# Ten instead of eight feed-forward sums begun in PSUM by VectorE, with new engine orders

## The reference

```
x = x + attn(ln(x))        # q = x Wq'; (q x') x, no softmax
x = x + ffn(ln(x))         # "f1"
x = x + rwkv(ln(x))        # time mix and channel mix
x = x + ffn(ln(x))         # "f2", the same weights as f1

ffn(t):   h = relu(t @ w1[0] + b1[0]);  y = t + h @ w2[0] + b2[0];  return ln(y) * gamma + beta
rwkv(x):  xa = ln(x); k, v, r = mixes of xa with its shift by one token, times Wk, Wv, Wr
          out = sigmoid(r) * wkv(k, v);  u = x + out @ Wo
          xc = ln(u); kk = relu(mix(xc) @ FWk)**2
          return u + sigmoid(mix(xc) @ FWr) * (kk @ FWv)
```

## Time and profile before

| | |
|---|---|
| Time, median of three runs | 259.4 us (259.05 to 259.99) |
| The profiled execution's own time | 259.21 us |
| Its span, first to last instruction | 257.4 us |
| PE busy | 249.5 us, 97% |
| DVE busy | 231.2 us, 90% |
| ACT busy | 231.9 us, 90% |
| POOL busy | 133.2 us, 52% |
| Granted TensorE clock, mean | 0.997 |

### The profile page before, as it was taken

One profiled execution on the slowest core, in us unless ns is written; L12 is line 12 of the kernel. 1 busy time (PEld: TensorE's weight loads), 2 busy tenths in 40 slices (PEclk: granted clock), 3 DMA queues, 4 the chain that ended last, 5 costly groups with the idle time before them and its releaser, 6 DMA issues.

```text
span 257.4 us, 5284 instructions
## 1 busy us (share of the span) xinstructions
PE 249.5 (97%) x1504; PEld 187.8 (73%) x1504; DVE 231.2 (90%) x757; ACT 231.9 (90%) x477; POOL 133.2 (52%) x258
## 2 busy tenths in 40 slices
PE   7899999999999999999999999999999999999991
PEld 7687778768767777668759767757848849778771
DVE  5897999999999999999999999999999995955454
ACT  3789789999999999999999999999999999895741
POOL 1656585944961974044596646636604525340640
PEclk9999999999999999999999999999999999999998
DMA  7932224013022240020763422205204424374297
GB/s 196 308 99 45 42 42 84 0 28 56 3 40 43 41 84 1 0 45 0 134 105 52 74 48 45 42 0 98 67 0 85 81 56 70 55 144 87 45 187 179
DMA packets 17772, 18.10 MB, mean 70 GB/s; under 512 B 1488, under 2 KB 11600, under 8 KB 17744
## 3 DMA queue, kind: packets, MB, share of 16 engines
q0 software_dynamic: 6480, 11.80, 27.0%
q1 hardware_dynamic: 10848, 5.84, 8.1%
q10 hardware_dynamic: 416, 0.14, 0.2%
HBM read 3.87 MB, written 2.10 MB: 23 GB/s over the span
## 4 chain that ended last, share of the span: by engine, by line
PE 94%; DVE 2%; DMA 1%; ACT 1%; POOL 1%; issue 0%; DVEq 0%; POOLq 0%; ACTq 0%
PE bank L1155 21%; PE bank L1164 21%; PE bank L1232 11%; PE bank L1226 11%; PE bank L1114 7%; PE bank L1213 3%; PE bank L1243 3%; PE bank L1197 3%; PE bank L1207 3%; PE bank L1202 3%; PE bank L1142 3%; PE bank L1127 2%; PE bank L1275 1%; DMA R<-in_hidden 1%; PE bank L1175 1%; PE bank L1135 1%
## 5 line engine op out<-in xcount | busy, mean ns | idle before, releaser
L1164 PEld LDWEIGHTS bank<-W,f_h 128*128 128x128 f32 x480 | 58.2, 192 | 8.7 <-issue 8.6
L1155 PE MATMUL bank<-f_yT,W 128*128 128x512 f32 x128 | 61.2, 593 | 0.0
L1164 PE MATMUL bank<-W,f_h 128*128 128x128 f32 x480 | 60.2, 275 | 0.0
L1155 PEld LDWEIGHTS bank<-f_yT,W 128*128 128x128 f32 x128 | 21.9, 190 | 16.3 <-issue 11.3
L1232 PEld LDWEIGHTS bank<-FWv,KK 128*128 128x128 f32 x256 | 30.6, 192 | 3.4 <-issue 2.3
L1226 PE MATMUL bank<-XK,FWk 128*128 128x512 f32 x64 | 32.0, 597 | 0.0
L1232 PE MATMUL bank<-FWv,KK 128*128 128x128 f32 x256 | 31.8, 275 | 0.0
L828 ACT ACTIVATE f_y<-R,f_yn_nb,f_yn_rs 128x128 f32<-128x128 f32 x64 | 26.3, 490 | 0.9 <-POOL f_yn_nb L350 0.9
L895 ACT ACTIVATE f_h<-bank,B 128x512 f32<-128x512 f32 x32 | 21.2, 681 | 5.5 <-PE bank L1155 4.2
L390 POOL DMA_DIRECT2D R<-G x7 | 6.3, 897 | 36.4 <-DVE G L686 36.4
L895 ACT ACTIVATE f_h<-bank,B1C 128x512 f32<-128x512 f32 x32 | 21.4, 682 | 0.1
(11 more groups left out here) (159 smaller groups left out, 620.3 us busy)
## 6 DMA issues: line engine op xcount, KB each, us to landing
R<-BETA POOLq DMA_DIRECT2D x16, 256.0 KB, 3.6
R<-f_zg POOLq DMA_DIRECT2D x14, 256.0 KB, 4.0
R<-N POOLq DMA_DIRECT2D x8, 256.0 KB, 3.4
R<-in_hidden SPq DMA_DIRECT2D x7, 256.0 KB, 5.0
R<-G POOLq DMA_DIRECT2D x7, 256.0 KB, 3.4
out_x<-R SPq DMA_DIRECT2D x7, 256.0 KB, 2.3
W<-in_w SPq DMA_DIRECT2D x2, 256.0 KB, 4.5
BETA<-in_beta SPq DMA_DIRECT2D x1, 256.0 KB, 4.6
```

The costliest lines, as they stand in the source:

```text
L1155: t_.matmul(banks[bank][:], W1[:, n * P:(n + 1) * P], at(f.yT, b)[:], start=True, stop=True).then_inc(f.h_psum[n], 1)
L1164: last = t_.matmul(banks[bank][:, j * C:(j + 1) * C], at(f.h, b)[:, n, j * P:(j + 1) * P], W2[:, n, :], start=False, stop=(n == H - 1), sk ...
```

## The change

`STARTED` gains batch 4 of f1 and batch 3 of f2. So DVE begins ten of the sixteen sums: batches 0 to 4 of f1 and 3 to 7 of f2, the last of them in two halves as before. PE does six `ffn_start` instead of eight. All four written-out lists are new in order, in bank numbers and in the waits for free banks; apart from the two moved `ffn_start` they hold the same calls as before. Two helpers are defined (`norm_bias` on DVE, `norm_log` on ACT) that no list calls. Cut to the lines that the prediction speaks of:

```diff
-STARTED = {"f1": (0, 1, 2, 3), "f2": (4, 5, 6, 7)}
+STARTED = {"f1": (0, 1, 2, 3, 4), "f2": (3, 4, 5, 6, 7)}
...
-            power(1, f1.norm); bias(1, f1.norm); shift(4, na); shift(5, na); power(4, na); ffn_residual(0, f1)
-            bias(4, na); shift(2, f1.norm); power(2, f1.norm); ffn_residual(1, f1); power(5, na); bias(2, f1.norm)
+            power(1, f1.norm); shift(4, na); bias(1, f1.norm); ffn_residual(0, f1); power(4, na); shift(2, f1.norm)
+            ffn_residual(1, f1); power(2, f1.norm); shift(5, na); bias(4, na); bias(2, f1.norm); power(5, na)
...
-            ffn_out(0, f1); tmix_stats(0); mean_var(0, nt); attn_out(3, 2); decay_along_tokens(); ffn_stats(3, f1)
+            mean_var(4, na); bias_rows_centred(); attn_stats(5); attn_out(2, 3); attn_stats(6); decay_along_tokens()
+            ffn_start(0, f1, 1); ffn_stats(2, f1); mean_var(2, f1.norm); ffn_start(1, f1, 0, (f1.h_ready[0], 1))
+            mean_var(5, na); z_stats(0, f1, 1); mean_var(0, f1.znorm); ffn_gain(0, f1, 1); ffn_out(0, f1)
+            tmix_stats(0); mean_var(0, nt); attn_stats(7); attn_out(3, 5); ffn_stats(3, f1); mean_var(6, na)
...
+            ffn_start(4, f1, 2); first_values(1, 4); numerator_sum(1); denominator_sum(1); attn_out(6, 5); weighted(1)
...
+            gate_sum(6); z_stats(1, f2, 5); mix_v(7); gate_log(6, 2); running_max(7, 1); mean_var(1, f2.znorm)
+            cmix_gated(4, 0); gated(6); ffn_start(3, f2, 2, square[2].done(5, "relu")); differences(7, 1)
...
-            attn_transpose(0, 0); attn_gram(0, 1); attn_proj(0, 1); attn_apply(0, 1); attn_transpose(1, 0)
+            attn_gram(0, 0); attn_transpose(0, 1); attn_proj(0, 0); attn_apply(0, 0); attn_transpose(1, 1)
...
+            product_v(6, 6); cmix_down(4, 0, 0); ffn_down(2, f2, 0, 7); product_r(6, 2); ffn_down(2, f2, 1, 7)
+            ffn_down(2, f2, 2, 7); cmix_transpose(5, 4); cmix_down(4, 1, 0); tmix_transpose(7, 6, (m2_ready, 7))
+            cmix_down(4, 2, 0); cmix_down(4, 3, 0); ffn_down(2, f2, 3, 7); cmix_up(5, 1, 6, (xa_ready, 8))
+            cmix_up(5, 3, 3, cgate.done(4, "rl")); cmix_up(5, 0, 4)
+            ffn_transpose(3, f2, 6, square[1].done(5, "relu")); product_k(7, 1); cmix_up(5, 2, 2, gate.done(6, "rl"))
...
+            product_o(7, 4, square[1].done(6, "relu")); gate_product(6, 6, square[3].done(6, "relu"))
+            hidden_up(4, f2, 3, 0, square[2].done(6, "relu")); cmix_down(6, 0, 4, (u1_ready, 8)); cmix_down(6, 1, 4)
+            cmix_down(6, 2, 4); ffn_down(4, f2, 0, 5); cmix_down(6, 3, 4); cmix_transpose(7, 6, cgate.done(6, "rl"))
+            ffn_down(4, f2, 1, 5); ffn_down(4, f2, 2, 5); ffn_down(4, f2, 3, 5); cmix_up(7, 2, 0)
```

More of the change, by code:

```diff
@@ L769, in _ @@
[L769 to L787, removed]
-            gated(3); cgate_log(1, 6); differences(4, 2); cmix_change(2); mean_var(6, f1.znorm); tmix_stats(5)
@@ L804, in _ @@
-            cmix_stats(6); cmix_r(5); mean_var(6, ncm); ffn_stats(4, f2); mix_r(7); ffn_scaled(1, f2, 6)
-            mean_var(4, f2.norm); new_values(7, 2); denominator_sum(7); numerator_sum(7); first_values(7, 2)
-            cmix_change(6); z_stats(2, f2, 1); cmix_k(6); weighted(7); with_current(7); gate_sum(7); cgate_log(5, 5)
-            gate_log(7, 4); cmix_gated(5, 0); gated(7); cmix_r(6); ffn_start(4, f2, 2, (f2.h_ready[0], 5))
-            mean_var(2, f2.znorm); tmix_out(7, 6); cmix_stats(7); mean_var(7, ncm); ffn_stats(5, f2)
@@ new lines, in _ @@
+            numerator_sum(2); first_values(2, 4); attn_out(7, 6); mean_var(4, f1.znorm); mean_var(1, ncm); weighted(2)
+            ffn_stats(7, f1); with_current(2); mean_var(7, f1.norm); tmix_change(3); gate_sum(2); mix_k(3)
+            ffn_scaled(4, f1, 2); cgate_log(0, 7); gate_log(2, 5); running_max(3, 6); gated(2); cmix_change(1)
+            differences(3, 6); tmix_stats(4); cmix_gated(0, 3); mean_var(4, nt); cmix_k(1); z_stats(5, f1, 1)
+            tmix_out(2, 3); mean_var(5, f1.znorm); mix_v(3); cmix_r(1); denominator_sum(3); mix_r(3); new_values(3, 3)
@@ new lines, in _ @@
+            ffn_stats(0, f2); cmix_stats(2); numerator_sum(3); mean_var(2, ncm); first_values(3, 3); weighted(3)
+            mean_var(0, f2.norm); with_current(3); tmix_change(4); gate_sum(3); cgate_log(1, 5); mix_v(4)
+            gate_log(3, 7); mix_k(4); ffn_scaled(5, f1, 1); z_stats(6, f1, 0); running_max(4, 5); gated(3)
+            mean_var(6, f1.znorm); differences(4, 5); cmix_change(2); tmix_stats(5); cmix_k(2); cmix_gated(1, 3)
+            mean_var(5, nt); mix_r(4); tmix_out(3, 4); cmix_r(2); ffn_scaled(6, f1, 0); cmix_stats(3)
@@ new lines, in _ @@
+            mean_var(4, f2.norm); new_values(7, 4); ffn_scaled(1, f2, 5); first_values(7, 4); denominator_sum(7)
+            numerator_sum(7); weighted(7); with_current(7); cmix_change(6); cmix_k(6); gate_sum(7); cgate_log(5, 3)
+            gate_log(7, 6); cmix_gated(5, 0); gated(7); cmix_r(6); tmix_out(7, 4); cmix_stats(7); mean_var(7, ncm)
+            z_stats(2, f2, 7); ffn_start(4, f2, 5, (f2.h_ready[0], 5)); z_stats(3, f2, 2); cgate_log(6, 6)
+            ffn_stats(5, f2); mean_var(2, f2.znorm); mean_var(5, f2.norm); cmix_change(7); cmix_k(7); cmix_gated(6, 4)
```

440 lines of the change are left out of this document (221 added, 219 removed).

## The result

The kernel before was timed at 259.4 us, the changed one at 260.49 us (260.32 to 260.86). The ratio is 1.0049, with a 95% interval of 1.0026 to 1.0072: slower by about 0.5%, that is 1.1 us. The forecast was 259.7, with a range of 258.5 to 260.9. The range holds the time, but the likeliest case (259.2 to 260.2) does not: 260.49 lies where the prediction had put its slower rival, whose mechanism did not happen.

What follows compares the result with a forecast made beforehand. DVE was taken to set the pace to about 208 us, then PE. DVE's +0.01 at gate_log(6) and PE's remaining work gave 0.19 to 0.45 later, taken as +0.3: median 259.4 to 259.7, range 258.5 to 260.9.

Steps and rivals of the forecast that it cites:

- the likeliest case: Handover of DVE to PE at gate_log(6) decides: +0.3 on 259.21, spanning 259.2 to 260.2; chance 0.57.
- DVE sets the pace to 208 us, PE behind it: Up to about 208 us DVE sets the pace, PE behind by a hair; from there PE alone.
- The decisive wait: cmix_up(5, 2) on PE takes bank 2 and waits for gate_log(6) on DVE; forecast to start at 189.96.
- When DVE gets there, +0.01: DVE work ahead of gate_log(6), from z_stats at 25.91: 0.58 + 0.28 - 0.52 - 0.33 = +0.01; ends about 189.9 again.
- POOL "is passed by nothing urgent": POOL, busy half the span, and its moved DMA issues cost 0; uncovered, one late issue below 1 us once.
- Neighbours at 0.11: DVE statistics followed by their own mean_var take 0.90, otherwise 0.79; three fewer pairs ahead of gate_log(6) save 0.33.
- What PE has left, 61.52 and 0 to 0.26 more: PE's work from cmix_up(5, 2) to last_down(0): 61.52 us instead of 63.08, plus 0.26 if a wait stays.
- Tail "nil": After PE's last calls: the same calls in another order, DVE having room; no change in time.
- The rival of the last channel mix: Slower rival: the chain from product_o(7) to cmix_up(7), margin 0.3, makes PE wait between 218 and 224; 260.9; chance 0.29.
- The rival in which PE's saving arrives: Faster rival: PE's 0.88 us comes out whole, 258.3 in the profile, 258.5 as a median; chance 0.14.
- ACT's copies: Two ffn_evacuate become copies, 585 for 686 ns, 0.2 us off ACT; price nil, at most -0.2 us.
- the new waits of the begun sums: The two moved DVE sums stand 0.5 and 2.5 us of work before the first ffn_down needing them; nil.

Runs made afterwards that it cites:

- e11: Kernel before, own orders, sums of batch 4 of f1 and batch 3 of f2 begun by nobody: eight transposes less on PE, nothing more on DVE; 259.28 us.
- e12: Kernel before, own orders, sums of batch 4 of f1 and batch 3 of f2 begun on DVE, PE's transposes kept; 260.78 us.
- e8: e6 with the sum of batch 4 of f1 back on PE, that of batch 3 of f2 still on DVE; 259.17 us.
- e10: e8 with the sum of batch 3 of f1 on PE too; 259.44 us.
- e1: Changed kernel with one swap in POOL's order: bias(1, nt) ahead of shift(7, na); 260.53 us.
- e3: e2 plus e1's POOL swap, and ffn_scaled(2, f2) ahead of ffn_stats(6, f2) on DVE; 259.47 us.
- e2: Changed kernel with tmix_stats(1) and mean_var(1, nt) ahead of ffn_stats(4, f1) on DVE, POOL's order unchanged; 259.56 us.
- e6: e3 plus a fourth move: cmix_sum(1) ahead of shift_twice(5) on POOL; 259.20 us.
- e7: e6 with both sums (batch 4 of f1, batch 3 of f2) back on PE; 259.44 us.

## Why the prediction was right or wrong, point by point

- **DVE sets the pace to 208 us, PE behind it: right.** e11 and e12 show it in the old orders: 0.88 off PE is worth 0, 1.16 on DVE costs 1.0. In the new orders the traces show it only while DVE has both sums: with one or two of them on PE, DVE waits at 74 to 84 us (e8, e10) and its saved time does not arrive.
- **The decisive wait: right in place, wrong in time.** `cmix_up(5, 2)` follows `gate_log(6)` by 0.06, at 191.59 instead of 189.96. Every later comparison could be made at this place. Of the other signs named, `last_down(0)` ends at 253.64 and not near 251.6, DVE is not full to 190 us, and PE's wait at 208.86 did vanish.
- **When DVE gets there, +0.01: this is the step that failed.** It compared only the work in DVE's list and took for granted that no new wait arises in it. Counted from `z_stats` at 25.91 (25.88 after) it is +1.65. Of that, the wait for batch 1's norm is 1.16 and that for `cmix_sum(1)` 0.25. What is left behind `tmix_change(0)` is 1.50 - 1.41 = 0.09, for which the prediction's own terms say 0.58 - 0.33 = 0.25; so the count of the work was sound to 0.2 us there. The other wrong term is -0.52 + 0.28 = -0.24 for the stretch up to `tmix_change(0)`: it measured +0.15 (9.71 against 9.56). What `decay_along_tokens` left free turned into waits, the largest before `ffn_out(0)`, and the count of neighbours missed the new pair of `attn_out(3)` and `ffn_stats(3)`, 31.91 - 31.19 = 0.72 where the first takes 0.60 ahead of other work; the lists give two such pairs less, not three. Timeline of DVE after:

```profile
28.06 1.14 DVE L552 SCALAR_TENSOR_TENSOR R<-f_zg,f_zn_rs,R 128x128 f32<-128x128 f32 x4 [0.30 <-ACT f_zn_rs L1030]
...
31.19 0.68 DVE L535 TENSOR_TENSOR R<-bank,R 128x512 f32<-128x512 f32 x1
31.91 0.87 DVE L441 BATCH_NORM_STATS2 f_yn_stats<-R 128x6 f32<-128x128 f32 x4
```

- **POOL "is passed by nothing urgent", priced 0, "below 1 us once" uncovered: wrong.** Both waits above come over POOL. The busy share of 52% said nothing about them: one is a scale held by DVE's own scans, the other an issue behind one that waited. The second, 0.25, is within the bound that the prediction gave for one late issue; the first, 1.16, is over it, and most of it is no late issue at all (e1: 0.3 for the step ahead of the bias). Both were called uncovered and left out of the range's reasons.
- **Neighbours at 0.11: the price holds.** In the changed kernel `tmix_stats` of batch 1, with other work behind it, takes 44.70 - 43.93 = 0.77:

```profile
43.93 0.86 DVE L441 BATCH_NORM_STATS2 tmix_stats<-R 128x6 f32<-128x128 f32 x4
44.70 0.67 DVE L613 TENSOR_TENSOR EV<-EB,bank 128x512 f32<-128x512 f32 x1
```

In e3, with its own `mean_var` behind it, 43.97 - 43.06 = 0.91. The sentence "the semaphore costs nothing extra here" of the Trainium skill (VectorE: DVE Perf Modes, The DRAIN you can't avoid), cited in the prediction, is measured there on chained copies; these statistics with their `mean_var` do not follow it:

```profile
43.06 0.87 DVE L441 BATCH_NORM_STATS2 tmix_stats<-R 128x6 f32<-128x128 f32 x4
43.97 0.38 DVE L524 BATCH_NORM_AGGREGATE tmix_mv<-tmix_stats 128x2 f32<-128x6 f32 x4
```

- **What PE has left, 61.52 and 0 to 0.26 more:** e2 and e6 have 62.51 from the start of `gate_log(6)` to the end of `last_down(0)`, of which 0.68 + 0.06 are DVE's end and the handover; that leaves 61.77. The upper end was right; which small waits make the 0.25 was not sorted out. The changed kernel's own profile has 0.29 more, the long transfer of `cmix_sum(6)`.
- **Tail "nil": wrong, and in the change's favour.** Counted from the end of `last_down(1)`, it is 4.5 us in all nine profiles of the new orders and 5.2 to 5.7 in the five of the old. The predicted sum had no term for it. Without this 0.7 the change would have cost 1.8.
- **The rival of the last channel mix: did not happen.** No wait of PE over 0.05 stands before its transposes or its `cmix_up(7)`. The number that it gave, 260.9, came near the result by another mechanism, and the upper part of the range stood on this rival alone: that the range holds 260.49 is luck. **The rival in which PE's saving arrives:** true in the new orders for the second sum, 0.43 of its 0.44 (e7 and e8); in the old orders none of it arrives (e11).
- **ACT's copies, the new waits of the begun sums, the head:** no run isolates them. No wait for a begun sum shows in the changed kernel's list of waits.

## What to carry over

When a list of calls is permuted, comparing the work ahead of the decisive wait is half the job: go through the chains that pass over a lightly used engine, and see for each what runs beside it and what stands ahead of it in its queue. Two such places made 1.4 of the 1.65 us here. Moving work between two engines that are both full has the sign of the engine that rules at that place and in that order, so price it place by place: 0.44 us off PE for 0.58 on DVE gained 0.43 behind 190 us and about 0.1 ahead of it in the new orders, and the two moves together cost 0.8 in the old ones. And a wait seen in one profiled execution should be looked for in a second, before it is mended and before two traces are subtracted from each other.

## What the runs showed of the hardware

**POOL is held by DVE instructions with two large SBUF inputs.** In the fences above, a POOL step on 128 x 4 elements that takes 0.19 to 0.20 us takes 0.89 to 1.02 where it begins under a scan or a product of two SBUF tiles (L625, L632, L637), and it ends within 0.06 us of that instruction's end: 46.83 and 46.83, 49.99 and 49.93, 50.39 and 50.34. `power`, 1.00 to 1.01 alone, takes 1.81 where it begins under L632: it ends 0.80 after that scan's end at 48.22. Under statistics with one input, or where DVE's other operand lies in PSUM, POOL's steps keep their length (45.27 and 46.35 before). The kernel before has held steps too (1.15 us at 46.95, under its scan L619), but not on the way to batch 1's bias. The Trainium skill states this rule (GPSIMD Engine Reference, section Specifications: the SBUF interfaces are shared with VectorE, with contention for instructions "with two SBUF inputs"), and the traces agree. The prediction did not weigh it.

**The last store takes 3.0 us in one order and 2.2 in the other.** From the end of `last_down(1)` to the end of DVE's last instruction both kernels take 2.24 us. That instruction ends 3.0 us before the span's end in the old kernel (254.41 of 257.4) and 2.2 before it in the new one (256.76 of 259.0). The last piece of the chain of waits, before and then after:

```profile
254.15 0.26 DVE R L491
...
256.50 0.26 DVE R L492
```

The difference is in the SP queue, which issues the store of batch 6 (L240) and then the two halves of batch 7 (L267). Timeline of SP, before:

```profile
253.81 0.37 SPq L240 DMA_DIRECT2D out_x<-R  x1
254.23 0.51 SPq L267 DMA_DIRECT2D out_x<-R  x1
254.78 0.50 SPq L267 DMA_DIRECT2D out_x<-R  x1
```

After:

```profile
255.32 0.37 SPq L240 DMA_DIRECT2D out_x<-R  x1
256.26 0.37 SPq L267 DMA_DIRECT2D out_x<-R  x1
256.79 0.38 SPq L267 DMA_DIRECT2D out_x<-R  x1
```

Before, the store of batch 6 is issued 0.60 us ahead of DVE's end, the halves queue up behind it, and the last of them starts 254.78 - 254.41 = 0.37 after DVE's end. After, batch 6 goes 1.44 ahead of DVE's end, and the last half starts 0.03 behind it. That is 0.34 of the 0.75; the rest is in the transfer, 2.3 us from issue to landing before and 1.9 after. All five profiles of the old orders have issues of 0.49 to 0.51 and 2.2 to 2.4 to landing, all nine of the new 0.37 to 0.40 and 1.8 to 1.9. So a store issued close ahead of the last one goes with the longer tail. No run moves that store alone, so that it is the cause is likely but not shown.
